# Experts of the last stage on seven tiles of 128 rows in place of eight of 112

## The chip, the cores and the metric

The kernel runs on one core of one Trainium2 chip, as one program. The metric is the device time of one execution in microseconds (us), the median of several runs.

## The reference

Eight sequences of 112 rows of 1024 floats pass through four layers, each an attention step and a feed-forward step. Only the last layer matters here:

```python
# L3 attention step: features z = layernorm(x) are gathered along the 16 nearest points
gathered = take_along_axis(feat, flat_idx, axis=2)
out = einsum('bkm,k->bm', lap, affine_w) + affine_b[0]
x = x + tanh(g_xattn[3]) * out
# L3 feed-forward step: 8 experts of rank 64, the best 2 of each row, weighted
gate_probs = softmax(x @ gate_w.T)            # x is the layernorm of the rows here
weights, sel = top_k(gate_probs, 2); weights = weights / sum(weights)
for e in range(8):
    y = x @ lora_A[e].T @ lora_B[e].T
    out = out + w_full[:, e:e + 1] * y
x = x + tanh(g_ffn[3]) * out
```

The feed-forward step treats every row by itself, so it doesn't matter which rows lie in one tile.

## The kernel before

The stages follow one another with a barrier between them. The last one, `gather_experts` (from L2814), holds both steps of the last layer. Its engines each run a loop over rounds u = 0 to 161. A round u below 128 is one of the 16 neighbours of one of the eight sequences (b = u // 16, k = u % 16). In it:

- DVE makes a one-hot matrix two rounds ahead (`marked(u + 2)`, L3088) from a row of numbers that a DMA has spread over 123 partitions, and reduces the bank of this round (`kept(u)`, L3098). `mark(n)` below is the L3088 instruction of round n.
- PE looks up with 24 small matmuls (`looked`, L2940). Every fourth round it turns four results (`turned`, L2949) and ACT copies them out (L3010).
- Every 16 rounds the table of the next sequence is made (`tabled` on PE, L2928; `split` on DVE, L298 to L307).

The spread rows come in four chunks c = 0 to 3 of a sequence, two DMAs each (912 and 72 KB), all issued by SP (`load_spread`, L292). There are two buffers, so a chunk of sequence b is issued once the rounds of sequence b - 2 have read its place, and it is first read by mark(16b + 4c).

What a sequence has gathered goes to DRAM and back: ACT stores it (L3017, round 16b + 17) and loads it again (`back_load`, L3021, round 16b + 21). PE transposes it (`returned`, L2959, in round 27 for sequence 0 and in round 16b + 25 for the others), and DVE adds it to the rows (`update`, L3107) two rounds later.

Then the experts of a sequence m run in 22 steps t, placed in round 16(m + 1) + 12 + t among the lookups of the sequences behind it. Sequence 0 has its first five steps in rounds 30, 30, 31, 31, 32, so its experts span rounds 30 to 49. The steps are: statistics (t = 0, DVE L442), root (t = 0, ACT L450), shift (t = 2, DVE L3071 to L3075), normalised rows zm (t = 3, ACT L3026), eight transposes (t = 5, PE L673) and their copies zT (t = 6, ACT L682), the gate's matmuls with 8 moving columns (t = 7, PE L2966), the matmuls h with 512 (t = 7 to 10, PE L2966), maximum, exponential and weights of the experts (t = 8 to 10), h times weights (t = 11, DVE L3151), its transposes and copy hT (t = 13, 14), the matmuls o (t = 15 to 18, PE L2966), two additions to the rows (t = 18 and 20, DVE L3158) and the store of the rows to the output (t = 21, ACT L3044). Step 21 of m and step 5 of m + 1 fall in one round; in it and the next, ACT issues the store first and then copies zT.

An f32 matmul of the code is two PE instructions. Each engine runs its instructions in the order of the loop. POOL only numbers the experts once (L2918) and is idle afterwards. The x rows of sequence 4 are loaded by ACT in round 32 (L3051), behind the root and zm of sequence 0.

Of the kernel before, what the change touches and what calls it, by code (L numbers as in the profile page):

```python
# [22 lines left out]
P = 128  # L23
# [2798 lines left out]
def gather_experts(nc, C, banks, gate, gate_ffn, x_in, x_out, A, gather, early):  # L2822
# [14 lines left out]
    with ExitStack() as ctx:  # L2837
        s_ = Scope(nc, ctx, "points")
        s_.sems += early.loaded.values()
        s_.sems += [*gather.first_loaded, gather.weights_loaded]  # L2840
        rest_x, z = s_.sb("x", [Q, B - 1, D]), s_.sb("z", [Q, 2, NA * CH])
        x = [early.sb["x0"][:]] + [rest_x[:, b, :] for b in range(B - 1)]
        consts = early.sb["consts"]
        count = consts[:, 8:9]
        norm = Norm(s_, 4)
        shift = s_.sb("shift", [Q, 4, 1])
        wsel, part = gather.wsel, gather.part
# [5 lines left out]
        gT, aT, bT = early.sb["gT"], gather.aT, gather.bT  # L2853
        zm, zT = s_.sb("zm", [Q, D]), s_.sb("zT", [P, KC, Q])
        prob, best, w8, hit = (s_.sb(n, [Q, NE]) for n in ("prob", "best", "w8", "hit"))
        place, placef, number = s_.sb("place", [Q, 8], U32), s_.sb("placef", [Q, 8]), s_.sb("number", [Q, NE])
        nmax, both = s_.sb("nmax", [Q, 1]), s_.sb("both", [Q, 1])
        h, hT = s_.sb("h", [Q, RE]), s_.sb("hT", [P, RE // P, Q])

# [7 lines left out]
        zm_ready, zT_ready, max_ready, prob_ready, h_ready, hT_ready, x_done = (  # L2867
            s_.sem(n) for n in ("zm_ready", "zT_ready", "max_ready", "prob_ready", "h_ready", "hT_ready", "x_done"))

        def steps(u):  # L2870
# [7 lines left out]

        order, nth = [], {}
        for u in range(ROUNDS):  # L2880
            b, k = u // K, u % K
            if u < U:
                order.append((("look", u), u % 3))
            if k % 4 == 1 and 1 < u <= U + 1:
                order.append((("turn", u // 4 - 1), 3))
            for m in returns(u):
                order += [(("back", m, i), 6 + i) for i in range(2)]
            if k == 13 and b + 1 < B:
                order.append((("table", b + 1), 6))
            if k == 2 and b + 1 < B:  # L2890
                nth["points", b + 1] = len(nth)
            for m, t in steps(u):
                if t == 0:
                    nth["experts", m] = len(nth)
# [21 lines left out]
        @block.gpsimd  # L2916
        def _(pool):
            pool.iota(number[:], pattern=[[1, NE]], base=0, channel_multiplier=0,  # L2918
                      allow_small_or_imprecise_dtypes=True).then_inc(numbered, 1)

        @block.tensor
        def _(pe):
# [39 lines left out]
            def part_of(t, lhsT, w, ks, n):  # L2962
                if ks[0] == 0:
                    pe.wait_ge(turns.free(t), turns.count(t, 0))
                for k in ks:
                    mm = pe.matmul(turns.tile(t)[0:Q, 0:n], lhsT[:, k, :], w(k), start=(k == 0), stop=(k == lhsT.shape[1] - 1))  # L2966
                if ks[-1] == lhsT.shape[1] - 1:
                    mm.then_inc(turns.full(t), 1)

            def experts(m, t):  # L2970
                if t == 5:
                    if m == 0:
                        pe.wait_ge(early.loaded["gT"], 16)
                        pe.wait_ge(gather.weights_loaded, 32)
                    pe.wait_ge(zm_ready, m + 1)
                    turn_rows(pe, C, turns, zm, "zT", m, 0)
                if t == 7:
                    pe.wait_ge(zT_ready, m + 1)
                    part_of(("gate", m), zT, lambda k: gT[:, k, :], list(range(KC)), NE)
                if 7 <= t < 11:  # L2980
                    part_of(("h", m), zT, lambda k: aT[:, k, :], [2 * (t - 7), 2 * (t - 7) + 1], RE)
                if t == 13:
                    pe.wait_ge(h_ready, m + 1)
                    turn_rows(pe, C, turns, h, "hT", m, 0, n=1)
                if t == 15:
                    pe.wait_ge(hT_ready, m + 1)
                if 15 <= t < 19:
# [18 lines left out]
        def _(act):  # L3006
# [16 lines left out]

            def scaled(out, src, i, n, ready):
                act.wait_ge(shift_ready, n + 1)
                act.activation(out, src, ACT.Identity, bias=shift[:, i, :], scale=norm.rstd[:, i, :]).then_inc(ready, 1)  # L3026

            def experts(m, t):
                i, n = 2 + m % 2, nth["experts", m]
                if t == 0:  # L3030
                    norm.root(act, i, n)
                if t == 3:
                    scaled(zm[:], x[m], i, n, zm_ready)
                if t == 6:
                    copy_turned(act, turns, zT, "zT", m, 0, zT_ready)
                if t == 9:
                    act.wait_ge(max_ready, m + 1)
                    act.activation(prob[:], turns.tile(("gate", m))[0:Q, 0:NE], ACT.Exp, bias=nmax[:]).then_inc(turns.free(("gate", m)), 1)
                    act.drain().then_inc(prob_ready, 1)
                if t == 14:  # L3040
                    copy_turned(act, turns, hT, "hT", m, 0, hT_ready, n=1)
                if t == 21:
                    act.wait_ge(x_done, m + 1)
                    act.dma_start(x_out[m], x[m]).then_inc(x_stored, 16)  # L3044

            for b in (1, 2):
                act.dma_start(x[b], x_in[b]).then_inc(x_loaded[b], 16)
            for u in range(ROUNDS):
# [5 lines left out]
                if k == 3 and b + 1 < B:  # L3054
                    norm.root(act, (b + 1) % 2, nth["points", b + 1])
                if k == 5 and 1 <= b <= B:
                    back_load(b - 1)
                if k == 6 and b + 1 < B:
                    scaled(z[:, (b + 1) % 2, 0:D], x[b + 1], (b + 1) % 2, nth["points", b + 1], z_ready)
                for m, t in steps(u):  # L3060
                    experts(m, t)
            act.wait_ge(x_stored, 16 * B)

        @block.vector
        def _(dve):
            def statistics(b, i):
                norm.statistics(dve, x[b], i)

            def shifted(i, n):
                dve.wait_ge(norm.std_ready, n + 1)  # L3070
# [3 lines left out]
                                         op0=ALU.mult, op1=ALU.mult)  # L3074
                dve.drain().then_inc(shift_ready, 1)  # L3075

# [25 lines left out]
            def update(b):  # L3102
                for i in range(2):
# [5 lines left out]
                       .then_inc(turns.free(t), 1)  # L3109
                dve.drain()  # L3110

            def weighed(m):
                dve.wait_ge(prob_ready, m + 1)
                dve.tensor_reduce(both[:], prob[:], AX, ALU.add)
# [12 lines left out]
                dve.drain()  # L3127
                dve.tensor_scalar(best[:, 0:2], best[:, 0:2], both[:], C.gates[0:Q, gate_ffn:gate_ffn + 1], ALU.mult, ALU.mult)
                dve.drain()
# [6 lines left out]
            def experts(m, t):  # L3136
                i, n = 2 + m % 2, nth["experts", m]
                if t == 0:
                    statistics(m, i)
                if t == 2:  # L3140
                    shifted(i, n)
                if t == 8:
                    g = ("gate", m)
                    dve.wait_ge(turns.full(g), turns.count(g, 0))
                    dve.tensor_reduce(nmax[:], turns.tile(g)[0:Q, 0:NE], AX, ALU.max, negate=True).then_inc(max_ready, 1)
                if t == 10:
                    weighed(m)
                if t == 11:
                    g = ("h", m)
                    dve.wait_ge(turns.full(g), turns.count(g, 0))  # L3150
                    dve.tensor_tensor(h[:].rearrange("q (e r) -> q e r", e=NE), turns.tile(g)[0:Q, :].rearrange("q (e r) -> q e r", e=NE),  # L3151
                                      w8[:].unsqueeze(2).broadcast_to([Q, NE, RANK]), ALU.mult).then_inc(turns.free(g), 1)
                    dve.drain().then_inc(h_ready, 1)
                if t in (18, 20):
                    g = ("o", m, (t - 18) // 2)
                    c = slice((t - 18) * 256, (t - 18) * 256 + 512)
                    dve.wait_ge(turns.full(g), turns.count(g, 0))
                    dve.tensor_tensor(x[m][:, c], turns.tile(g)[0:Q, :], x[m][:, c], ALU.add).then_inc(turns.free(g), 1)  # L3158
                    if t == 20:
# [7 lines left out]
            for u in range(ROUNDS):  # L3167
# [5 lines left out]
                if k == 2 and b + 1 < B:  # L3173
                    dve.wait_ge(x_loaded[b + 1], 16)
                    statistics(b + 1, (b + 1) % 2)
                if k == 5 and b + 1 < B:
                    shifted((b + 1) % 2, nth["points", b + 1])
                for m in returns(u - 2):
# [121 lines left out]
```

## Time and profile before

| | us |
|---|---|
| median of 3 runs | 2813.17 |
| lowest, highest | 2810.91, 2819.49 |
| span of the profiled execution | 2820.8 |
| the last stage in it | from 2479 to the end |

For the profiled execution the profile gives no time of its own beside its span; the span is above all three runs' times. Shares of the span in it: PE 92%, PEld 65%, DVE 68%, ACT 38%, POOL 20%. These are averages over stages with different limits, so the last stage has to be read by itself: by its stretches, by the chain that ended last, by DVE's timeline and by what the DMA queue of SP had moved at given moments. Times in the views are us from the start of the span.

### The profile page before, as it was taken

Reading aid. Unit: us, or ns where it says so; the run is one execution under the profiler, and the core shown is the slowest. Engines: PE = TensorE matmul, PEld = TensorE weight load, DVE = VectorE, ACT = ScalarE, POOL = GpSimd, SP = SyncE. Lnnn points to the kernel's source line nnn. Section 1 sums busy time; section 2 is a strip of 40 time slices with the busy share of each in tenths; the row PEclk is TensorE's granted clock in tenths of the full one; section 3 lists DMA queues with packets and bytes.
Section 4 is the critical chain, followed back from the end, with each engine's and each line's share of the span. In section 5 each row is a group of like instructions: output and inputs, shape, how many; then the busy total and the mean of one; then the engine's idle time right before and its main releaser. Section 6 shows DMA issues by size and latency. Waiting matters only on the chain. (4 is left out here: it accounts for less than half of the span.)

```text
span 2820.8 us, 48283 instructions
## 1 busy us (share of the span) xinstructions
PE 2583.5 (92%) x18264; PEld 1842.1 (65%) x18268; DVE 1907.7 (68%) x3366; ACT 1080.2 (38%) x2605; POOL 564.3 (20%) x602
## 2 busy tenths in 40 slices
PE   7999999999999699998899999998688999868888
PEld 5856855855865388885555555555487788556664
DVE  6376376366467677774578877777558889867774
ACT  3443434334345233332334444443255655302222
POOL 0110100001011300000045454455123334200000
PEclk9999999999999899997899999998799999989999
DMA  8011010111110745556275666544240010544421
GB/s 325 2 38 59 1 59 23 38 35 47 38 60 32 255 112 149 145 160 218 111 238 168 176 172 172 166 133 113 71 186 9 24 46 24 140 143 170 168 96 39
DMA packets 154483, 307.64 MB, mean 109 GB/s; under 512 B 84000, under 2 KB 107200, under 8 KB 144760
## 3 DMA queue, kind: packets, MB, share of 16 engines
q1 hardware_dynamic: 128952, 232.78, 25.6%
q0 software_dynamic: 19376, 57.15, 6.6%
q10 hardware_dynamic: 5936, 14.75, 1.8%
q8 instruction: 141, 2.31, 0.3%
q14 instruction: 78, 0.64, 0.1%
HBM read 249.53 MB, written 42.52 MB: 104 GB/s over the span
## 5 line engine op out<-in xcount | busy, mean ns | idle before, releaser
L1758 DVE TENSOR_REDUCE latent_nmax<-bank 112x1 f32<-112x487 f32 x128 | 85.0, 666 | 242.3 <-PE bank L1561 235.9
L1458 POOL TENSOR_SCALAR latent_probs<-latent_probs,latent_rsum 112x487 f32<-112x487 f32 x128 | 88.1, 688 | 789.6 <-DVE latent_rsum L1763 789.6
L2190 POOL TENSOR_SCALAR grouped_probs<-grouped_probs,grouped_rsum 112x375 f32<-112x375 f32 x256 | 169.6, 680 | 279.4 <-DVE grouped_rsum L2246 279.4
L2457 PE MATMUL bank<-ffn_qT,gather_whole 128*128 128x128 bf16 x3584 | 207.1, 220 | 16.7 <-ACT ffn_us L2580 6.7
L2457 PEld LDWEIGHTS bank<-ffn_qT,gather_whole 128*128 128x128 fp8e4 x3584 | 203.1, 98 | 21.7 <-issue 20.5
L2640 POOL TENSOR_TENSOR ffn_h<-ffn_sl,ffn_us 128x512 f32<-128x512 f32 x56 | 127.4, 2275 | 278.0 <-ACTq L2583 278.0
L2137 ACT ACTIVATE grouped_probs<-bank,grouped_nmax 112x375 f32<-112x375 f32 x256 | 143.3, 573 | 76.4 <-DVE grouped_nmax L2242 76.3
L2242 DVE TENSOR_REDUCE grouped_nmax<-bank 112x1 f32<-112x375 f32 x256 | 122.3, 540 | 72.2 <-PE bank L2048 69.9
L2940 PEld LDWEIGHTS bank<-gather_part,points_onehot 123*128 123x128 bf16 x3072 | 111.9, 103 | 63.1 <-DVE points_onehot L3088 32.6
L2184 POOL TENSOR_SCALAR grouped_raw<-grouped_raw,grouped_rscale 128x1024 f32<-128x1024 f32 x96 | 120.5, 1274 | 144.3 <-DVEq L2220 144.2
L2057 PEld LDWEIGHTS bank<-const_ident,grouped_probs 112*125 112x125 f32 x768 | 105.1, 196 | 67.4 <-DVE grouped_probsT L2254 28.8
L1508 PE MATMUL bank<-latent_zT,front_wq 128*128 128x224 f32 x768 | 148.0, 353 | 0.0
L1533 PE MATMUL bank<-latent_wo,latent_oT 128*128 128x512 f32 x336 | 146.6, 592 | 0.0
L1508 PEld LDWEIGHTS bank<-latent_zT,front_wq 128*128 128x128 f32 x768 | 145.0, 190 | 1.9 <-issue 1.8
L2940 PE MATMUL bank<-gather_part,points_onehot 123*128 123x63 bf16 x3072 | 117.5, 200 | 30.0 <-DVE points_onehot L3088 26.3
L2057 PE MATMUL bank<-const_ident,grouped_probs 112*125 112x112 f32 x768 | 109.8, 282 | 24.8 <-DVE grouped_probsT L2254 18.8
L1468 PE MATMUL bank<-front_wkv,front_cT 128*125 128x384 f32 x384 | 127.0, 491 | 0.0
L1468 PE MATMUL bank<-front_cT,front_wkv 128*128 128x375 f32 x384 | 123.3, 478 | 0.0
L1693 ACT ACTIVATE latent_probs<-bank,latent_nmax 112x487 f32<-112x487 f32 x128 | 85.5, 668 | 89.9 <-DVE latent_nmax L1758 82.4
L2573 ACT ACTIVATE ffn_sl<-ffn_gs,ffn_sgu 128x128 f32<-128x128 f32 x224 | 71.6, 390 | 116.5 <-DVEq L2703 116.1
L1520 PE MATMUL bank<-latent_probsT,latent_v 125*96 125x224 f32 (+1 forms) x512 | 110.2, 358 | 4.1 <-DVEq L1777 4.1
L1533 PEld LDWEIGHTS bank<-latent_wo,latent_oT 128*128 128x128 f32 x336 | 63.2, 190 | 73.9 <-issue 73.7
(435 smaller groups left out, 5576.0 us busy)
## 6 DMA issues: line engine op xcount, KB each, us to landing
grouped_raw<-L_weights SPq DMA_DIRECT2D x24, 2048.0 KB, 9.0
points_spread<-numbers SPq DMA_DIRECT2D x16, 912.0 KB
codes<-grouped_flip SPq DMA_DIRECT2D x24, 512.0 KB, 2.6
front_cT<-ctxT SPq DMA_DIRECT2D x8, 1500.0 KB, 6.8
plain_ctxT<-ctxT POOLq DMA_DIRECT2D x8, 1500.0 KB, 22.5
plain_ctx<-ctx POOLq DMA_DIRECT2D x8, 1500.0 KB, 23.4
grouped_ctx<-ctxT SPq DMA_DIRECT2D x8, 1500.0 KB, 6.7
gather_whole<-numbers SPq DMA_DIRECT2D x12, 912.0 KB
```

Source lines behind the costliest of these rows:

```text
L1468: mm = pe.matmul(turns.tile(t)[0:m, 0:n], lhsT(k), rhs(k), start=(k == 0), stop=(k == KC - 1))
L1508: mm = pe.matmul(turns.tile(t)[:, c * 2 * Q:(c + 1) * 2 * Q], wq[:, k, (2 * i + c) * P:(2 * i + c + 1) * P], zT[:, k].rearrange("p s q -> ...
L1520: mm = pe.matmul(turns.tile(t)[0:HD, 2 * half * Q:2 * (half + 1) * Q], v[0:n, k, g * HD:(g + 1) * HD], pT[0:n, half, k], start=(k == 0), s ...
L1533: mm = pe.matmul(turns.tile(t)[:], oT[:, (b - 1) % 2, k, :], wo[:, k, i * 512:(i + 1) * 512], start=(k == 0), stop=(k == OC - 1))
L2057: mm = pe.transpose(turns.tile(t)[0:CT, j * Q:(j + 1) * Q], pr[:, g % 2, j, k * CT:(k + 1) * CT], C.ident[0:Q, 0:Q])
L2137: act.activation(pr[:, i, j, :], turns.tile(t)[0:Q, 0:CTX], ACT.Exp, bias=nmax[:, i, j:j + 1], accum_out=rsum[:, i, j:j + 1]).then_inc(tur ...
L2184: pool.tensor_scalar(w, w, rscale[:, slot, i % m:i % m + 1], MAGIC, ALU.mult, ALU.add).then_inc(raw_scaled, 1)
L2190: pool.tensor_scalar(pr[:, g % 2, j, :], pr[:, g % 2, j, :], rsum[:, g % 2, j:j + 1], 1.0, ALU.mult, ALU.mult)\
L2242: dve.tensor_reduce(nmax[:, g % 2, j:j + 1], turns.tile(t)[0:Q, 0:CTX], AX, ALU.max, negate=True).then_inc(max_ready, 1)
L2457: mm = pe.matmul(ahead.tile(t)[:, i * P:(i + 1) * P], wgu[:, u0 + f // 4, c:c + 2 * P - 1:2], qT[:, k, :], start=(k == 0), stop=(k == KC - 1))
L2640: pool.tensor_tensor(h[:, G * j:G * j + G, :], sl[:, j % 2], us[:, j % 2], ALU.mult).then_inc(h_ready, 1)
L2940: mm = pe.matmul(turns.tile(t)[:, j * RA:(j + 1) * RA], onehot[0:ROWS, u % 3, j * P:(j + 1) * P], part[n][0:ROWS, b % 2, :], start=(n == 0 ...
```

## The change

The experts of sequence 0 have no steps of their own any more. Each of the seven other tiles gets 128 partitions: 112 rows of its own sequence and, in partitions 112 to 127, 16 rows of sequence 0. Once sequence 0 has its update (round 29), POOL issues seven DMAs that copy its rows there, SBUF to SBUF, 64 KB each. DVE waits for all seven ahead of the statistics of m = 1 in round 44. All operations of the experts are 128 rows wide instead of 112. Each tile is stored with two DMAs instead of one. The normalisation has buffers of its own for the experts; what the semaphores count is adapted.

```diff
-        rest_x, z = s_.sb("x", [Q, B - 1, D]), s_.sb("z", [Q, 2, NA * CH])
+        rest_x, z = s_.sb("x", [P, B - 1, D]), s_.sb("z", [Q, 2, NA * CH])
+        full = [None] + [rest_x[:, b, :] for b in range(B - 1)]
-        norm = Norm(s_, 4)
+        norm, wide = Norm(s_, 2), Norm(s_, 2, P, "wide")
-            return [(m, t) for m in range(B) for t in range(22)
-                    if u == ((30, 30, 31, 31, 32)[t] if m == 0 and t < 5 else 16 * (m + 1) + 12 + t)]
+            return [(m, t) for m in range(1, B) for t in range(22) if u == 16 * (m + 1) + 12 + t]
         @block.gpsimd
+            pool.wait_ge(first_done, 1)
+            for m in range(1, B):
+                pool.dma_start(full[m][Q:P], x[0][(P - Q) * (m - 1):(P - Q) * m]).then_inc(rows_moved, 16)
         part_of:
-                    mm = pe.matmul(turns.tile(t)[0:Q, 0:n], lhsT[:, k, :], w(k), ...)
+                    mm = pe.matmul(turns.tile(t)[0:P, 0:n], lhsT[:, k, :], w(k), ...)
-                    turn_rows(pe, C, turns, zm, "zT", m, 0)
+                    turn_rows(pe, C, turns, zm, "zT", m, 0, rows=P)
         ACT, t == 21:
                     act.dma_start(x_out[m], x[m]).then_inc(x_stored, 16)
+                    act.dma_start(x_out[0][(P - Q) * (m - 1):(P - Q) * m], full[m][Q:P]).then_inc(x_stored, 16)
         DVE, update:
-                dve.drain()
+                if b == 0:
+                    dve.drain().then_inc(first_done, 1)
+                else:
+                    dve.drain()
         DVE, experts, t == 0:
-                    statistics(m, i)
+                    if m == 1:
+                        dve.wait_ge(rows_moved, 16 * (B - 1))
+                    wide.statistics(dve, full[m], i)
```

## Rows read from the trace of the kernel before

**Rows 1.** Busy time by stretch: us, PE, PEld, DVE, ACT, POOL (instructions), clock, DMA.

```profile
2479.28:2530.40 51.12, 36.05 (x774) 32.97 (x774) 38.59 (x80) 7.03 (x11) 0.14 (x1) 0.85 0.50 164
2530.40:2543.79 13.39, 9.78 (x118) 8.98 (x119) 8.77 (x20) 1.70 (x3) 0.00 (x0) 0.56 0.41 149
2702.84:2740.02 37.18, 33.47 (x486) 23.95 (x486) 29.08 (x68) 9.50 (x14) 0.00 (x0) 1.00 0.19 60
```

**Rows 2.** The chain that ended last: start, us, what; two transfers, then the tail.

```profile
2487.55 37.97 DMA points_spread<-numbers
...
2554.43 10.16 DMA points_back<-flat
...
2796.45 0.33 ACTq L3044
2796.83 0.54 ACT points_zT L682
```

**Rows 3.** DMA queue q1 (SP's): packets, MB from 2484.6 to 2533.4, 2544.8, 2564.7.

```profile
q1 hardware_dynamic: 817, 5.96, 35.6%
q1 hardware_dynamic: 1033, 7.55, 36.3%
q1 hardware_dynamic: 1330, 9.70, 35.4%
```

**Rows 4.** The same queue in 2566 to 2582 and in 2582 to 2604.

```profile
q1 hardware_dynamic: 307, 2.25, 38.2%
q1 hardware_dynamic: 338, 2.47, 30.8%
```

**Rows 5.** DVE's timeline: start, us, what, count, idle before it and its releaser.

```profile
2533.39 0.48 DVE L3088 TENSOR_SCALAR points_onehot<-gather_whole,points_consts 123x1024 bf16<-123x1024 bf16 x1 [0.79 <-DMA gather_whole<-numbers]
2538.91 1.29 DVE L442 BATCH_NORM_STATS2 points_ln_stats<-points_x 112x6 f32<-112x512 f32 x2
2540.63 0.48 DVE L3088 TENSOR_SCALAR points_onehot<-gather_whole,points_consts 123x1024 bf16<-123x1024 bf16 x1
2564.69 0.49 DVE L3088 TENSOR_SCALAR points_onehot<-gather_whole,points_consts 123x1024 bf16<-123x1024 bf16 x1
2568.65 0.68 DVE L3098 TENSOR_REDUCE points_val<-bank 128x56 f32<-128x504 f32 x1 [3.47 <-PE bank L2940]
2579.42 0.68 DVE L3098 TENSOR_REDUCE points_val<-bank 128x56 f32<-128x504 f32 x1 [1.77 <-PE bank L2940]
2581.86 0.69 DVE L3158 TENSOR_TENSOR points_x<-bank,points_x 112x512 f32<-112x512 f32 x1
```

**Rows 6.** ACT's timeline around the first store of gathered rows of sequence 1.

```profile
2529.21 0.59 ACT L3010 ACTIVATE points_flat<-bank 56x512 f32<-56x512 f32 x1 [8.54 <-PE bank L2949]
...
2542.30 0.31 ACTq L3051 DMA_DIRECT2D points_x<-x  x1
2544.21 0.32 ACTq L3017 DMA_DIRECT2D flat<-points_flat  x1
```

**Rows 7.** PE's timeline: the gate's matmuls and h of sequence 1.

```profile
2588.05 1.72 PE L2966 MATMUL bank<-points_gT,points_zT 128*112 128x8 f32 x16
2589.62 1.95 PE L2966 MATMUL bank<-gather_whole,points_zT 128*112 128x512 f32 x4
```

**Rows 8.** PE instructions by line, ns min/median/max: 112 and 128 stationary columns.

```profile
L2966 PEld LDWEIGHTS bank<-gather_whole,points_zT x128: 176/177/310, 2548.4 to 2805.6; 128*112 128x112 f32 x128
L2966 PE MATMUL bank<-gather_whole,points_hT x128: 592/592/815, 2569.6 to 2815.2; 128*112 128x512 f32 x128
L1533 PEld LDWEIGHTS bank<-latent_wo,latent_oT x336: 187/190/192, 211.6 to 918.8; 128*128 128x128 f32 x168
L1533 PE MATMUL bank<-latent_wo,latent_oT x336: 590/592/608, 211.7 to 919.2; 128*128 128x512 f32 x168
```

**Rows 9.** The dearest kind of DMA issue on POOL (1.5 MB each), ns min/median/max.

```profile
L755 POOL DMA_DIRECT2D plain_ctx<-ctx x8: 1307/1319/1342, 976.4 to 1242.7; - x8
```

**Rows 10.** The way back of gathered rows (L3021, 448 KB), from issue to landing.

```profile
DMA to landing us min/median/max: 3.1/9.0/10.2
```

More of the change, by code:

```diff
@@ L2840, in gather_experts @@
         s_.sems += [*gather.first_loaded, gather.weights_loaded]
-        rest_x, z = s_.sb("x", [Q, B - 1, D]), s_.sb("z", [Q, 2, NA * CH])
-        x = [early.sb["x0"][:]] + [rest_x[:, b, :] for b in range(B - 1)]
+        rest_x, z = s_.sb("x", [P, B - 1, D]), s_.sb("z", [Q, 2, NA * CH])
+        x = [early.sb["x0"][:]] + [rest_x[0:Q, b, :] for b in range(B - 1)]
+        full = [None] + [rest_x[:, b, :] for b in range(B - 1)]
         consts = early.sb["consts"]
         count = consts[:, 8:9]
-        norm = Norm(s_, 4)
-        shift = s_.sb("shift", [Q, 4, 1])
+        norm, wide = Norm(s_, 2), Norm(s_, 2, P, "wide")
+        shift, wide_shift = s_.sb("shift", [Q, 2, 1]), s_.sb("wide_shift", [P, 2, 1])
         wsel, part = gather.wsel, gather.part
@@ L2853, in gather_experts @@
         gT, aT, bT = early.sb["gT"], gather.aT, gather.bT
[L2854 to L2858, printed above, removed]
+        zm, zT = s_.sb("zm", [P, D]), s_.sb("zT", [P, KC, P])
+        prob, best, w8, hit = (s_.sb(n, [P, NE]) for n in ("prob", "best", "w8", "hit"))
+        place, placef, number = s_.sb("place", [P, 8], U32), s_.sb("placef", [P, 8]), s_.sb("number", [P, NE])
+        nmax, both = s_.sb("nmax", [P, 1]), s_.sb("both", [P, 1])
+        h, hT = s_.sb("h", [P, RE]), s_.sb("hT", [P, RE // P, P])
         numbered = s_.sem("numbered")
@@ L2889, in gather_experts @@
                 order.append((("table", b + 1), 6))
-            if k == 2 and b + 1 < B:
-                nth["points", b + 1] = len(nth)
             for m, t in steps(u):
-                if t == 0:
-                    nth["experts", m] = len(nth)
                 if t == 5:
@@ L2965, in part_of @@
                 for k in ks:
-                    mm = pe.matmul(turns.tile(t)[0:Q, 0:n], lhsT[:, k, :], w(k), start=(k == 0), stop=(k == lhsT.shape[1] - 1))
+                    mm = pe.matmul(turns.tile(t)[0:P, 0:n], lhsT[:, k, :], w(k), start=(k == 0), stop=(k == lhsT.shape[1] - 1))
                 if ks[-1] == lhsT.shape[1] - 1:
@@ L2982, in experts @@
                 if t == 13:
-                    pe.wait_ge(h_ready, m + 1)
-                    turn_rows(pe, C, turns, h, "hT", m, 0, n=1)
+                    pe.wait_ge(h_ready, m)
+                    turn_rows(pe, C, turns, h, "hT", m, 0, n=1, rows=P)
                 if t == 15:
-                    pe.wait_ge(hT_ready, m + 1)
+                    pe.wait_ge(hT_ready, m)
                 if 15 <= t < 19:
@@ L3022, in back_load @@
                               flat_dram[b % 2].rearrange("a c -> (a c)").rearrange("(p c) -> p c", p=P)).then_inc(back_loaded[b % 2], 16)
-            def scaled(out, src, i, n, ready):
-                act.wait_ge(shift_ready, n + 1)
-                act.activation(out, src, ACT.Identity, bias=shift[:, i, :], scale=norm.rstd[:, i, :]).then_inc(ready, 1)
             def experts(m, t):
-                i, n = 2 + m % 2, nth["experts", m]
+                i = m % 2
                 if t == 0:
-                    norm.root(act, i, n)
+                    wide.root(act, i, m - 1)
                 if t == 3:
-                    scaled(zm[:], x[m], i, n, zm_ready)
+                    act.wait_ge(wide_shift_ready, m)
+                    act.activation(zm[:], full[m], ACT.Identity, bias=wide_shift[:, i, :], scale=wide.rstd[:, i, :]).then_inc(zm_ready, 1)
                 if t == 6:
-                    copy_turned(act, turns, zT, "zT", m, 0, zT_ready)
+                    copy_turned(act, turns, zT, "zT", m, 0, zT_ready, rows=P)
                 if t == 9:
-                    act.wait_ge(max_ready, m + 1)
-                    act.activation(prob[:], turns.tile(("gate", m))[0:Q, 0:NE], ACT.Exp, bias=nmax[:]).then_inc(turns.free(("gate", m)), 1)
+                    act.wait_ge(max_ready, m)
+                    act.activation(prob[:], turns.tile(("gate", m))[0:P, 0:NE], ACT.Exp, bias=nmax[:]).then_inc(turns.free(("gate", m)), 1)
                     act.drain().then_inc(prob_ready, 1)
                 if t == 14:
-                    copy_turned(act, turns, hT, "hT", m, 0, hT_ready, n=1)
+                    copy_turned(act, turns, hT, "hT", m, 0, hT_ready, n=1, rows=P)
                 if t == 21:
-                    act.wait_ge(x_done, m + 1)
+                    act.wait_ge(x_done, m)
                     act.dma_start(x_out[m], x[m]).then_inc(x_stored, 16)
+                    act.dma_start(x_out[0][(P - Q) * (m - 1):(P - Q) * m], full[m][Q:P]).then_inc(x_stored, 16)
             for b in (1, 2):
@@ L3054, in _ @@
                 if k == 3 and b + 1 < B:
-                    norm.root(act, (b + 1) % 2, nth["points", b + 1])
+                    norm.root(act, (b + 1) % 2, b)
                 if k == 5 and 1 <= b <= B:
@@ L3058, in _, with shifted @@
                 if k == 6 and b + 1 < B:
-                    scaled(z[:, (b + 1) % 2, 0:D], x[b + 1], (b + 1) % 2, nth["points", b + 1], z_ready)
+                    i = (b + 1) % 2
+                    act.wait_ge(shift_ready, b + 1)
+                    act.activation(z[:, i, 0:D], x[b + 1], ACT.Identity, bias=shift[:, i, :], scale=norm.rstd[:, i, :]).then_inc(z_ready, 1)
                 for m, t in steps(u):
                     experts(m, t)
-            act.wait_ge(x_stored, 16 * B)
+            act.wait_ge(x_stored, 2 * 16 * (B - 1))
         @block.vector
         def _(dve):
-            def statistics(b, i):
-                norm.statistics(dve, x[b], i)
-            def shifted(i, n):
+            def shifted(norm, shift, ready, i, n):
                 dve.wait_ge(norm.std_ready, n + 1)
@@ L3127, in weighed @@
                 dve.drain()
-                dve.tensor_scalar(best[:, 0:2], best[:, 0:2], both[:], C.gates[0:Q, gate_ffn:gate_ffn + 1], ALU.mult, ALU.mult)
+                dve.tensor_scalar(best[:, 0:2], best[:, 0:2], both[:], C.gates[:, gate_ffn:gate_ffn + 1], ALU.mult, ALU.mult)
                 dve.drain()
@@ L3136, in experts @@
             def experts(m, t):
-                i, n = 2 + m % 2, nth["experts", m]
+                i = m % 2
                 if t == 0:
-                    statistics(m, i)
+                    if m == 1:
+                        dve.wait_ge(rows_moved, 16 * (B - 1))
+                    wide.statistics(dve, full[m], i)
                 if t == 2:
-                    shifted(i, n)
+                    shifted(wide, wide_shift, wide_shift_ready, i, m - 1)
                 if t == 8:
@@ L3144, in experts @@
                     dve.wait_ge(turns.full(g), turns.count(g, 0))
-                    dve.tensor_reduce(nmax[:], turns.tile(g)[0:Q, 0:NE], AX, ALU.max, negate=True).then_inc(max_ready, 1)
+                    dve.tensor_reduce(nmax[:], turns.tile(g)[0:P, 0:NE], AX, ALU.max, negate=True).then_inc(max_ready, 1)
                 if t == 10:
@@ L3150, in experts @@
                     dve.wait_ge(turns.full(g), turns.count(g, 0))
-                    dve.tensor_tensor(h[:].rearrange("q (e r) -> q e r", e=NE), turns.tile(g)[0:Q, :].rearrange("q (e r) -> q e r", e=NE),
-                                      w8[:].unsqueeze(2).broadcast_to([Q, NE, RANK]), ALU.mult).then_inc(turns.free(g), 1)
+                    dve.tensor_tensor(h[:].rearrange("q (e r) -> q e r", e=NE), turns.tile(g)[0:P, :].rearrange("q (e r) -> q e r", e=NE),
+                                      w8[:].unsqueeze(2).broadcast_to([P, NE, RANK]), ALU.mult).then_inc(turns.free(g), 1)
                     dve.drain().then_inc(h_ready, 1)
@@ L3157, in experts @@
                     dve.wait_ge(turns.full(g), turns.count(g, 0))
-                    dve.tensor_tensor(x[m][:, c], turns.tile(g)[0:Q, :], x[m][:, c], ALU.add).then_inc(turns.free(g), 1)
+                    dve.tensor_tensor(full[m][:, c], turns.tile(g)[0:P, :], full[m][:, c], ALU.add).then_inc(turns.free(g), 1)
                     if t == 20:
@@ L3174, in _ @@
                     dve.wait_ge(x_loaded[b + 1], 16)
-                    statistics(b + 1, (b + 1) % 2)
+                    norm.statistics(dve, x[b + 1], (b + 1) % 2)
                 if k == 5 and b + 1 < B:
-                    shifted((b + 1) % 2, nth["points", b + 1])
+                    shifted(norm, shift, shift_ready, (b + 1) % 2, b)
                 for m in returns(u - 2):
```

12 lines of the change are left out of this document (6 added, 6 removed).

## The prediction

> **What bounds the kernel now.** I read the stage from its start on 2479 by stretches, then the chain, then DVE's timeline and SP's queue.
>
> PE is the busiest engine of the last stage: 33.5 of 37.2 us in a full period of 16 rounds with experts, DVE 29.1 beside it [rows 1]. Neither is full, but they hand work to each other every round, so the period is long by both. From this view the experts of one sequence look like a big prize. They are 16 h and 16 o instructions and 16 gate instructions. The gate takes 2589.62 - 2588.05 = 1.57 us for 16 [rows 7]; a big one is spaced 0.45 us (four last 1.95, one alone 0.59 [rows 7, 8], so three spacings are 1.36), which makes 32 x 0.45 + 1.6 = 16 us, and about 1.5 us for 12 transposes: some 17.5 us of PE.
>
> The experts of sequence 0 don't lie in such a period, though. They lie in rounds 30 to 49, from 2538.91 [rows 5] to shortly before the gate of sequence 1 at 2588.05 [rows 7], and that stretch has another limit. The first third of the stage is led by the spread rows: the chain holds a transfer of 38 us [rows 2], PE was busy 36.1 of 51.1 us [rows 1], and mark(32) at 2533.39 still waited for its chunk [rows 5]. A chunk is 123 rows of 8 KB, 1.01 MB. When mark(32) was let go, five chunks had landed, 5.04 MB, and q1 had moved 5.96 MB [rows 3]: the queue runs 0.92 MB ahead of what is complete. From there to 2564.7 it moved 9.70 - 5.96 = 3.74 MB in 31.3 us [rows 3], 0.12 MB/us, with its share of the engines constant at 35 to 36%. So the stream never pauses, and it can't be hurried by reading earlier.
>
> How far is the stream ahead of the marks? At 2544.8 (mark(36), chunk 6 needed, 6.05 MB) it stands 7.55 - 6.05 - 0.92 = 0.58 MB ahead, 4.8 us. At 2564.69 (mark(44), 8 chunks, 8.06 MB [rows 5]) it is 9.70 - 8.06 - 0.92 = 0.72 MB, 6 us [rows 3]. The lead within the queue may well be larger than 0.92 MB there, as it varies; with 1.2 MB these are 2.5 and 3.7 us. So the rounds that lose their experts can come forward by 3 to 6 us until round 42, and not more. Behind that the slack grows by itself, since a period with experts takes 37 us [rows 1] and its four chunks 4.03/0.12 = 34.
>
> **The change part by part.** Taken against the profiled execution, 2820.8 us of span, whose difference I then put on the median of the runs, 2813.2; the two differ by 7.6 us, which is the run and not a stage that I can name.
>
> *Removed in rounds 30 and 31.* DVE loses the statistics of sequence 0, 2540.63 - 2538.91 = 1.7 us [rows 5], and the shift. PE stands at 0.56 of its clock there, that is mostly at 1.2 GHz [rows 1], and a lookup then takes about 1.3 us, so only some 1.1 us reach the store of the gathered rows at 2544.21 [rows 6]. Without root and zm ahead of it the load of x rows at 2542.30 moves forward to ACT's last copy, near 2530, and away from that store [rows 6]. The way back of what was stored was issued at 2554.43 [rows 2], so the store had at most 10.2 us for its 448 KB. Transfers of that size took 3.1 to 10.2 us, the median 9.0 [rows 10]. With no neighbour of ACT's I take 8 for the store, from 2543.1 to 2551.1, and 9.0 for the way back: it lands at 2560.1 instead of 2564.6.
>
> *The stream's new neighbours.* In 2566 to 2582 q1 ran alone at 2.25/16 = 0.141 MB/us, in 2582 to 2604 with four transfers of ACT at 2.47/22 = 0.112 [rows 4]: 22 x 0.029 = 0.64 MB less, 1.1 us for each transfer of 448 KB. The seven DMAs of POOL are together one such transfer, and start before 2533, after the update that precedes mark(32) [rows 5]. The moved load of x is another for chunks 6 and 7. So chunk 8 lands 1.1 us later than now: mark(44) comes forward by 3.7 - 1.1 = 2.6 us, at most 4.9.
>
> *Rounds 42 to 49.* Now kept(42) comes at 2568.65, 3.5 us late for PE [rows 5], and 4.1 us after the way back has landed (2554.43 + 10.16 [rows 2]); of these some 0.8 are four transposes of h at the low clock, which go. So it comes at 2560.1 + 3.3 = 2563.4, right behind mark(44) at 2562.1: 5.2 us earlier. Behind it go the wait of 1.77 us at 2579.42 for the o matmuls, and two additions of 0.69 us with 0.14 of gap each [rows 5]: 5.2 + 1.8 + 1.7 = 8.7 us. Against it stands PE's clock, which falls after idle time; if it is at 1.2 GHz for a part of this, rounds of 1.22 us become 1.3 and the table is twice as dear. I take off 1.2: **7.5 us gained by round 50**, bounds 4 and 9.
>
> *128 rows instead of 112.* DVE's work doesn't change with partitions. The big matmuls cost the same, 592 ns at 112 and at 128 stationary columns [rows 8]. The gate is paced by its weight loads, 98 ns each; loads grow from 177 to 190 ns [rows 8], so 16 x 13 = 0.21 us per tile. Transposes move 16 more columns, 0.45 us/512 x 16 = 14 ns each by 12, of which half lie on the chain, 0.08. The copies of zT and hT grow from 448 columns in 0.54 us [rows 2] toward the 512 in 0.59 of another copy [rows 6], 0.05 each.
>
> *The second store.* It is one more issue of 0.33 us with a gap of 0.05 in ACT's queue, ahead of the copies of zT of the next tile. This lies on the chain: 2796.45 store, 2796.83 copy [rows 2], and in the periods too the gate waits for these copies. So m = 2 to 7 pay 0.38 + 0.10 on the way to the gate, m = 1 doesn't (no store is ahead of it). Sum per tile: m = 1 0.3; m = 2 to 5 0.78 each, 3.1; m = 6 and 7 in the tail, with nothing to hide behind, 0.9 each, 1.8; the last store 0.38. That is 5.6 us. In the periods PE also waits for DVE, which hides some; I take 4.8, bounds 3 and 6.
>
> *The move itself.* POOL has nothing else queued. Seven issues of 1.32 us, as the dearest were [rows 9], are 9.2 us, and a transfer of 448 KB is 9 [rows 10], so the move ends by 2552; DVE asks for it in round 44, near 2568. It costs nothing as long as those 16 us cover it. If they don't, DVE stands with every mark and kept of the later rounds behind the wait, and PE behind those.
> The rows show POOL's issues only at moments that don't tell how busy DVE's second port was. The Trainium skill (SBUF — State Buffer, "SBUF: two separate sides") says that descriptors of POOL's DMAs can't be written while DVE runs in a two-port mode, and names 620 ns growing to 3100. An estimate by that page is 7 x 3.1 = 22 us, which would still be hidden; no row here shows the blocking.
>
> **Sum:** 7.5 - 4.8 = 2.7 us less: 2818.1 of span, 2810.5 as median.
>
> **The rivals.**
> *The stream doesn't bind.* If it can be hurried or the lead is smaller, rounds 34 to 50 run at DVE's pace: 16 rounds in 29.1 us, its busy time in a full period [rows 1], less 3.5 for the part of the expert steps that goes, plus 3 of gaps, so 17 in 30.4. Now they take 43.3, from 2544.8 to 2588.05. That gains 13, less 4.8: 8.2, 2805.0. For it speaks PE's and DVE's load; against it the constant 35% of q1.
> *Nothing is left.* PE at 1.2 GHz through the thinned rounds (it had 0.56 in 2530 to 2544 [rows 1]) and all of the width's cost on the chain: 4 - 6, 2 us slower, 2815.
> *Slower: the move is late.* The wait in round 44 decides from 2568 on, 35 us after the update, or 5 us for each of the seven DMAs. Each us beyond is lost in full. With 8 us each (the descriptors starved between DVE's marks) it ends at 2588.6, 20 us late, 17 net: 2830. Against it: 1.32 us per issue at most [rows 9], and DVE idles a quarter of the stretch. The page named above is the rule behind this rival.
>
> **How the numbers follow.** Forecast 0.60; stream doesn't bind 0.17; nothing left 0.18; move late 0.05. Own range of the forecast, 4 - 6 to 9 - 3: 2807 to 2815. The range for 8 in 10 takes in most of the first rival and what the runs differ by: 2803.0 to 2816.5. Within 0.3% (8.4 us, about what a measurement of this kernel can tell from no change) lie the forecast and the third case. Faster by more: the first rival from its middle on and a tail of the forecast, 0.16. Slower by more: the late move and a bit, 0.06.
>
> **What would show it.** Right: mark(40) or mark(44) waits for a DMA of numbers; the way back of sequence 1 lands about 2559; the first gate starts 8 us before 2588; the gap between store and copy of zT holds a second issue; gates take 1.8 us; later periods are 0.5 to 0.8 us longer. Wrong: no DMA wait in rounds 34 to 46 and a start of the gate 12 us early (first rival); a PE clock of a half from 2550 to 2575; a wait of DVE before L442 of m = 1 for the row copies.

## The result and the profile after

The changed kernel is slower: 2827.9 us against 2818.7 (medians of 20 runs each), a ratio of 1.0035 with a 95% interval of 1.0023 to 1.0047. The forecast was 2.7 us less; it came out some 10 us more, 0.35%. The median before of 20 runs, 2818.7, is itself 5.5 us above the median of three runs, 2813.2, on which the prediction put its range of 2803.0 to 2816.5. So its times in us were set too low from the start; the difference between the kernels is what the rest is about.

The two profiles don't show this at first sight. The span of the profiled execution is 2819.0 us after and 2820.8 before. Single executions of either kernel lie within 21 to 25 us of each other (before 2807.3 to 2832.0, after 2819.6 to 2840.6), and here a quick execution of the changed kernel was caught beside a rather slow one of the old. So I give a second profile of each in the view that matters: the last stage cut into a front (from its start to the gate of m = 1), a middle (to the gate of m = 6) and a tail. Columns: stretch, us, busy us and instructions of PE, PEld, DVE, ACT, POOL, then clock, DMA share, GB/s.

The kernel before, the profile that the prediction read:

```profile
2479.36:2588.05 108.69, 84.63 (x1435) 71.16 (x1435) 78.08 (x171) 19.62 (x30) 0.14 (x1) 0.84 0.49 165
2588.05:2774.59 186.54, 165.76 (x2322) 118.23 (x2318) 138.88 (x322) 46.06 (x68) 0.00 (x0) 0.98 0.36 124
2774.59:2820.80 46.21, 37.78 (x120) 18.71 (x120) 12.96 (x42) 7.89 (x11) 0.00 (x0) 0.91 0.15 43
```

The kernel before, a second profile (e5 below), cut at the same gates:

```profile
2481.20:2583.70 102.50, 82.07 (x1435) 68.60 (x1435) 78.16 (x171) 19.63 (x30) 0.12 (x1) 0.86 0.51 172
2583.70:2766.40 182.70, 163.25 (x2322) 115.74 (x2317) 138.79 (x322) 46.07 (x68) 0.00 (x0) 1.00 0.37 128
2766.40:2812.50 46.10, 37.62 (x120) 18.71 (x120) 12.96 (x42) 7.89 (x11) 0.00 (x0) 0.91 0.16 44
```

The kernel after, its profile:

```profile
2477.53:2576.10 98.57, 67.37 (x1374) 62.78 (x1375) 71.95 (x148) 13.84 (x22) 3.55 (x8) 0.80 0.52 171
2576.10:2766.62 190.52, 167.66 (x2323) 120.69 (x2319) 138.03 (x322) 46.83 (x68) 0.00 (x0) 0.99 0.37 129
2766.62:2819.00 52.38, 43.16 (x120) 22.75 (x120) 12.94 (x42) 8.11 (x11) 0.00 (x0) 0.83 0.11 37
```

The kernel after, a second profile (e1 below):

```profile
2480.40:2583.30 102.90, 70.31 (x1374) 64.94 (x1374) 71.89 (x148) 13.83 (x22) 3.55 (x8) 0.78 0.53 166
2583.30:2775.20 191.90, 169.31 (x2319) 121.49 (x2316) 138.01 (x322) 46.84 (x68) 0.00 (x0) 0.98 0.37 128
2775.20:2824.80 49.60, 40.37 (x120) 20.91 (x120) 12.95 (x42) 8.11 (x11) 0.00 (x0) 0.88 0.12 39
```

The front went from 102.5 or 108.7 to 98.6 or 102.9 us, with 12 to 17 us less of PE's time busy in it: by these four alone it is shorter by up to 10 us or not at all. The middle went from 182.7 or 186.5 to 190.5 and 191.9, and the tail from 46.1 and 46.2 to 52.4 and 49.6. Nothing of the experts of sequence 0 was ever in these two. That is 4 to 9 us in the middle and 3 to 6 in the tail, though two profiles of each don't size it: single executions differ there too (table behind the experiments).

What grew there stands in ACT's timeline at the place that [rows 2] showed for before. After, from the store of gathered rows (L3017) to the copies of zT, ahead of the gate of m = 3:

```profile
2649.70 0.33 ACTq L3017 DMA_DIRECT2D flat<-points_flat  x1
2650.29 0.33 ACTq L3041 DMA_DIRECT2D x_final<-points_x  x1
2650.65 1.36 ACTq L3042 DMA_DIRECT2D x_final<-points_x  x1
2652.05 1.09 ACT L682 ACTIVATE points_zT<-bank 128x512 f32<-128x512 f32 x2 [2.46 <-issue]
```

The second store (L3042) holds ACT for 1.36 us, not for 0.33. Of all seven, first the two stores of a tile after (ns min/median/max of the issue), then the single one of before:

```profile
L3041 ACTq DMA_DIRECT2D x_final<-points_x x7: 322/328/1320, 2611.7 to 2814.6; - x7
L3042 ACTq DMA_DIRECT2D x_final<-points_x x7: 445/1357/1948, 2613.0 to 2814.9; - x7
```

```profile
L3044 ACTq DMA_DIRECT2D x_final<-points_x x8: 328/328/373, 2586.2 to 2816.6; - x8
```

In the first of the seven tiles it was the other way round: the first store took 1.32 us and the second 0.45. The other six second stores took 1.36, 1.62, 1.69 and 1.95 us, and 0.45 twice.

And the chain that ended last, after, where the tail begins:

```profile
2762.68 0.33 ACTq L3017
2763.05 0.37 ACTq L3041
2763.45 1.95 ACTq L3042
2765.40 0.05 issue
2765.45 0.60 ACT points_zT L682
2766.04 0.53 ACTq L684
2766.62 13.39 PE bank L2966 x32
```

The issue of 1.95 us lies on the chain, and PE waits for it: its waits for the drain behind the copies (L684) are 10.8 us in the stage, against 4.0 in before.

```profile
PE bank L2966 <- ACTq L684: 10.8, 8, 3.7
```

```profile
PE bank L2966 <- ACTq L684: 4.0, 4, 1.8
```

The tail after is granted 0.83 of the clock in one profile and 0.88 in the other, against 0.91 in both of before. How much of this follows from the waits is taken up below.

### The profile page after: what moved, and what is told of

The parts are those of the page before. It is cut to its first block and busy times, and to the rows that moved or that the text cites. A ratio compares the mean times of both kernels' runs of the same rounds, so it can differ in the third digit from the quotient of the medians.

```text
span 2819.0 us, 48123 instructions
## 1 busy us (share of the span) xinstructions
PE 2572.6 (91%) x18204; PEld 1838.7 (65%) x18208; DVE 1900.4 (67%) x3343; ACT 1074.0 (38%) x2597; POOL 566.0 (20%) x609
## 5 line engine op out<-in xcount | busy, mean ns | idle before, releaser
L3095 DVE TENSOR_REDUCE points_val<-bank 128x56 f32<-128x504 f32 x128 | 86.8, 678 | 39.0 <-PE bank L2940 38.8
```

## The experiments

Ratios are against the kernel before, run on the same chip in turn; 0.001 is 2.8 us. A difference in us behind a ratio is worked out from the ratio. e1 to e4 shared one chip, e5 to e8 a second, e9 to e12 a third.

**e1, the changed kernel again.**

> The changed kernel once more, as the yardstick for the other three and for a second profile. Issue theory (the second store of a tile stands in ACT's queue ahead of the copies of zT, with an issue of 1.3 to 2.0 us where 0.38 was reckoned): ratio about 1.003, again five issues of L3042 over 1.3 us, and a step of over 1.5 us from x_done to the first copy of zT for m = 3 to 6. Clock theory (the thinned rounds and the longer waits lower PE's clock): the ratio is the same, but the low-clock time of the last stage differs from profile to profile and the time goes with it.

Measured: 2826.2 us, 1.0029 (1.0015 to 1.0043). Its second stores took 0.81, 1.54, 1.71, 1.77, 1.95, 0.45 and 0.45 us to issue. So four lie over 1.3 us. I expected five "again", but the first profile had four at L3042 as well; its fifth slow one was a first store. The result of the first runs holds. The low-clock theory isn't excluded by this run alone.

**e2, the second store from POOL.**

```diff
-                    act.dma_start(x_out[0][...], full[m][Q:P]).then_inc(x_stored, 16)
+            for m in range(1, B):          # POOL, behind the move
+                pool.wait_ge(x_done, m)
+                pool.dma_start(x_out[0][...], full[m][Q:P]).then_inc(rows_stored, 16)
```

> The second store of each tile is issued by POOL, on a semaphore of its own, and no longer by ACT. Everything else as in the changed kernel, and the output is complete. Issue theory: the 0.45 + 4 x 1.5 us of issue leave ACT's queue; 6 to 8 us less than the changed kernel, about 2820, ratio to before 1.000. Clock or width theory: no change against the changed kernel, ratio 1.003.

Measured: 2818.2 us, 0.9993 (0.9980 to 1.0007). This interval lies apart from that of e1. Moving seven issues of 64 KB from one queue to another takes back 0.36%, 10 us by the ratios and 8 by the medians. One first store, still issued by ACT, took 1.36 us (m = 1, at 2622.75), with no second one behind it. POOL's issue is short every time, and the middle and the tail are near the size of e5's:

```profile
L2922 POOL DMA_DIRECT2D x_final<-points_x x7: 484/484/487, 2623.0 to 2811.6; - x7
```

```profile
2586.70:2769.90 183.20, 165.54 (x2319) 119.59 (x2316) 138.11 (x322) 46.85 (x68) 2.43 (x5) 1.00 0.38 134
2769.90:2817.20 47.30, 37.04 (x120) 18.68 (x120) 12.96 (x42) 8.11 (x11) 0.97 (x2) 0.92 0.16 46
```

**e3, no second store.** The line is left out, and POOL stores sequence 0 once after its update.

> The second stores are left out; sequence 0 is stored once by POOL straight after its update, so its rows in the output are without the experts' part. The move and the 128 rows stay. Issue theory: as with POOL's stores, 6 to 8 us below the changed kernel; what is between the two is the price of the transfers themselves, 0 to 1 us. Width theory: still at or above the kernel before.

Measured: 2815.5 us, 0.9993 (0.9978 to 1.0007), the same ratio as e2. The transfers cost nothing that shows; what cost was where they were issued. The profile is of the slowest of its twelve runs (2827.6) and is a warning: its middle is 193.0 us long without any second store, with two periods of over 41 us at a granted clock of 0.92.

**e4, the gain alone.** 112 rows everywhere, no move, no second store.

```diff
-        rest_x, z = s_.sb("x", [P, B - 1, D]), ...
+        rest_x, z = s_.sb("x", [Q, B - 1, D]), ...
-                turn_rows(pe, C, turns, zm, "zT", m, 0, rows=P)      # and so on for all experts' tiles
+                turn_rows(pe, C, turns, zm, "zT", m, 0)
+            pool.dma_start(x_out[0], x[0]).then_inc(rows_stored, 16)
```

> The experts of sequence 0 are simply left out (its rows in the output are without their part, stored once by POOL after the update); the seven other tiles stay at 112 rows, with no move and no second store. This is the gain alone. My sum: 7.5 us below the kernel before, 2811, ratio 0.997; bounds 4 and 9, and 13 if the stream of spread rows doesn't bind. The difference to the run without second stores is the width and the move: my sum 2 to 2.5 us. Clock theory: less than 4 us below before, with a low-clock time of the last stage 10 us above before's 55.

Measured: 2812.7 us, 0.9982 (0.9966 to 0.9998). The gain of leaving out an eighth of the experts is 5 us, with an interval from 0.6 to 9.6; the medians differ by 7.2. So neither my sum of 7.5 nor the clock theory's "less than 4" can be told from it. The front is 96.0 us in its profile, the middle 189.6. The expectation of 13 us if the stream of spread rows didn't bind is excluded by the interval.

**e5, the kernel before again, one run.**

> The kernel before, unchanged, for a second profile of it: when does the gate of m = 1 start, counted from the start of the last stage (109 us in the first profile, 96 to 103 in the four kernels without experts of sequence 0), and which periods hold a spell of low clock (41 us with one, 37 without)? Both theories expect 105 to 112 us and one or two long periods.

Measured: 2814.1 us in its one run. The gate of m = 1 starts 102.5 us into the stage, below the range that I expected, and no period is long. This suggests that the profile that the prediction read was an unlucky one in its front: 108.7 us. The other kernels with all eight tiles have 102.7 (e7), 105.4 (e8, which clears zm first), 102.7 (e10) and 102.5 (e12).

**e6, both stores behind the copies of zT.**

```diff
                 if t == 6:
                     copy_turned(act, turns, zT, "zT", m, 0, zT_ready, rows=P)
+                    if m > 1:
+                        stored(m - 1)        # the two stores of t == 21
```

> The changed kernel, complete, with both stores of a tile issued by ACT behind the two copies of zT of the next tile instead of ahead of them. Issue theory: the slow issue (1.4 to 2.0 us as the third transfer that ACT issues within a microsecond) no longer stands before the gate, so 7 to 10 us below the changed kernel, ratio to before 0.999. If the transfer itself is the cost (its share of the queue), nothing changes: 1.003.

Measured: 2813.3 us, 0.9987 (0.9969 to 1.0006). The same bytes go from the same queue, 1.2 to 1.4 us later, and 0.42% is back (against e1, on another chip; the intervals lie apart). It has the lowest ratio of the complete kernels, though its interval holds no change, and e2, e11 and e12 can't be told from it. Five of the seven second stores took 0.45 us, one 0.72 and one 1.62, though these two came about 2 us behind the store of gathered rows:

```profile
L3047 ACTq DMA_DIRECT2D x_final<-points_x x7: 450/451/1625, 2619.9 to 2806.9; - x7
```

**e7, a split store alone.** The kernel before, with one more issue per tile and nothing else.

```diff
-                    act.dma_start(x_out[m], x[m]).then_inc(x_stored, 16)
+                    act.dma_start(x_out[m][0:Q - 16], x[m][0:Q - 16]).then_inc(x_stored, 16)
+                    act.dma_start(x_out[m][Q - 16:Q], x[m][Q - 16:Q]).then_inc(x_stored, 16)
```

> The kernel before with the store of each tile as two DMAs, 96 and 16 rows, in ACT's queue where the one was; nothing else changes, the bytes and rows are the same. Issue theory: the second issue takes 1.4 to 2.0 us in the middle tiles, and the kernel is 8 to 10 us slower, ratio 1.003. If the width or the move was the cause: 1.000.

Measured: 2829.1 us, 1.0048 (1.0028 to 1.0068): 13.5 us for splitting eight stores (7.9 to 19.2). This is at least the loss of the changed kernel, within the noise, with none of its other parts. The second issues took 0.59, 0.83, 1.60, 2.71, 1.77, 2.02, 0.44 and 0.45 us: the first two are shorter than expected, the fourth is longer. ACT's timeline in the worst tile:

```profile
2697.49 0.33 ACTq L3017 DMA_DIRECT2D flat<-points_flat  x1
2698.11 0.33 ACTq L3044 DMA_DIRECT2D x_final<-points_x  x1
2698.47 2.71 ACTq L3045 DMA_DIRECT2D x_final<-points_x  x1
2701.23 0.98 ACT L682 ACTIVATE points_zT<-bank 128x448 f32<-128x448 f32 x2 [3.84 <-issue]
```

Its front is as before, its middle is 195.6 us long and its tail 47.1:

```profile
2478.10:2580.80 102.70, 80.41 (x1435) 67.03 (x1435) 78.36 (x171) 19.60 (x30) 0.14 (x1) 0.88 0.51 170
2580.80:2776.40 195.60, 168.81 (x2316) 119.43 (x2316) 138.42 (x322) 46.02 (x68) 0.00 (x0) 0.97 0.36 122
2776.40:2823.50 47.10, 37.92 (x120) 18.82 (x120) 12.95 (x42) 7.89 (x11) 0.00 (x0) 0.90 0.12 37
```

**e8, the width alone.** The kernel before, with zm, zT, prob, h and hT of 128 rows; all eight tiles are 128 wide from the transposes to the o matmuls.

> The kernel before with all experts 128 rows wide from the transposes on (rows 112 to 127 of zm are zero, the additions stay at 112 rows): eight tiles, the width alone. My sum: 0.3 to 0.45 us for each of eight tiles, 3 us, ratio 1.001. Width theory: 8 us or more, 1.003.

Measured: 2819.4 us, 1.0010 (0.9994 to 1.0025), 2.8 us, as summed, though the interval holds zero too. The loss of 10 us is outside of it.

**e9, the small store first.** The two lines of t = 21 change places.

> The changed kernel with the 64 KB store of a tile ahead of the 448 KB one; both stay ahead of the copies of zT. Issue theory, in the form that the third transfer issued by ACT in about a microsecond is the slow one whatever its size: the small store now takes 0.33 us and the big one behind it 1.4 to 2.0, and the ratio stays at 1.003. If the slow issue belongs to transfers of 16 rows, the small one stays slow in first place and the big one takes 0.4.

Measured: 2825.6 us, 1.0023 (1.0005 to 1.0042). The 64 KB store, now L3041, is quick, and the 448 KB store behind it is the slow one:

```profile
L3041 ACTq DMA_DIRECT2D x_final<-points_x x7: 321/327/373, 2613.8 to 2823.8; - x7
L3042 ACTq DMA_DIRECT2D x_final<-points_x x7: 439/1558/1772, 2614.1 to 2824.1; - x7
```

So it isn't the 16 rows: here the slow issue is the third of ACT's in a row, and not the small one. In all these kernels the last two tiles, which have no store of gathered rows right ahead, pay 0.44 or 0.45 us for the second one.

**e10, the move alone.**

```diff
+            pool.wait_ge(first_done, 1)
+            for m in range(1, B):
+                pool.dma_start(full[m][Q:P], x[0][...]).then_inc(rows_moved, 16)
```

> The kernel before with only the move added: POOL copies the rows of sequence 0 into partitions 112 to 127 of the seven other tiles after its update, and nothing reads them; DVE waits for the move ahead of the first addition to sequence 0, in round 46. My sum: the spread stream loses 1.1 us, hidden or nearly; ratio 1.000, at most 1.001. Late-move theory: 1.003 and more.

Measured: 2820.8 us, 1.0010 (0.9993 to 1.0026). In its profile (span 2810.4) DVE never waits for the move. The interval reaches from 2 us gained to 7 lost, so whether the move costs something these runs can't tell.

**e11, both stores from POOL.** As e2, with `pool.dma_start(x_out[m], x[m])` ahead of the other.

> The changed kernel, complete, with both stores of a tile issued by POOL. ACT issues no store any more and starts the copies of zT 0.4 us earlier than in the kernel before. Issue theory: the best of all, 0.38 us for each of six tiles below the run with only the second store on POOL: 2 us less, ratio 0.998 to 0.999. If POOL's transfers were starved by DVE, the last one would land late and the end would be 1 to 5 us later.

Measured: 2816.2 us, 0.9991 (0.9975 to 1.0007). POOL's issues took 0.50 to 0.55 us. The 2 us beyond e2 that were expected can't be told from the noise.

**e12, the kernel before with late stores.** As e6, for the one store of before.

> The kernel before with its single store of a tile behind the copies of zT of the next tile. It shows what moving the stores gives without the change of tiles: 0.38 us for each of seven tiles, 2 to 3 us, ratio 0.999. The changed kernel with late stores then stands against this one for the fewer tiles: my sum for that is 5 gained (the run without experts of sequence 0) less 3 for the width.

Measured: 2813.9 us, 0.9990 (0.9975 to 1.0005). It stands beside e6 (0.9987): with the stores out of the way in both, tiles of 128 rows and eight tiles of 112 can't be told apart. The difference that I had put at 2 us is there or not within the noise.

**All profiles side by side.** The kernels that have ACT issue two stores ahead of the copies of zT are the last four rows. Middle: from the gate of m = 1 to that of m = 6. Last period: from the gate of m = 5 to that of m = 6. Waits: PE at the gate and the o matmuls for ACT's drain (L684), in the whole stage.

| profile | middle, us | last period, us | waits, us |
|---|---|---|---|
| before, e5 | 186.5, 182.7 | 32.7, 32.7 | 4.0, 4.0 |
| e4, e10, e12 | 189.6, 183.5, 181.8 | 32.7, 32.7, 32.3 | 4.0, 4.0, 3.4 |
| e8, e2, e3 | 182.9, 183.2, 193.0 | 33.0, 33.0, 33.0 | 4.1, 4.7, 4.7 |
| e6, e11 | 183.3, 184.3 | 32.6, 32.6 | 3.5, 3.5 |
| after, e1 | 190.5, 191.9 | 35.0, 36.7 | 10.8, 10.5 |
| e7, e9 | 195.6, 197.6 | 34.8, 34.9 | 11.3, 10.7 |

The middle alone doesn't part the two kinds: e3 and e4 have long ones with no second store, in periods whose clock fell to 0.92 to 0.96. The waits and the last period do part them, in every profile: 6 to 8 us more of waits, and 1.8 us or more in the last period.

## Why the prediction was wrong

**The step that failed is "the second store".** The prediction found its place rightly: in ACT's queue, ahead of the copies of zT, with the gate behind them on the chain. It priced it wrongly, with the 0.33 us of an issue and a gap, taken from a row of a queue in which two transfers follow one another. Where a store of gathered rows had just been issued, the second store was the third issue in a row and mostly took 1.4 to 2.0 us. I had 0.38 for each of the stores, 2.7 us in all. Undoing it is worth 8 to 12 us (e1 or the first runs against e2), and adding it alone to the kernel before costs 13.5 (e7). The direct part is the issues themselves: the seven sum to 8.0 us in the profile after and to 8.7 in e1, six of them ahead of a gate, and PE's waits for ACT grew by 6 to 8 us. That a rest of some us is PE's clock, lower after the longer waits, is argued and not shown.

This also hit the range: it had a rival with the width's costs all on the chain, but none in which an issue costs more than every issue of its kind in the trace. The bounds for a new operation were taken from its like, not from what surrounds it. The trace of before had a warning in another queue: SP's issues of spread rows, one behind the other, took from 0.26 to 11.2 us each, eight of them 3.44 us at the start of the stage and the next eight 33.7.

```profile
L292 SPq DMA_DIRECT2D points_spread<-numbers x32: 258/502/8549, 2484.6 to 2693.5; - x32
L292 SPq DMA_DIRECT2D gather_whole<-numbers x24: 295/2291/11222, 2488.1 to 2655.0; - x24
```

**The gain in the front may have been too big.** The sum had 7.5 us with bounds 4 and 9; e4 measures 5 (0.6 to 9.6), which holds both. The limit was seen rightly. In the profile after, mark(40) and mark(44) wait for their chunks, 0.21 and 4.22 us, as the working had said of the stream. All eight profiles without experts of sequence 0 have such a wait at mark(44), 3.3 to 4.2 us, and none of the six with them has one. In the profile after PE also waits 7.07 us for the way back, and DVE behind it for PE:

```profile
2544.77 0.49 DVE L3085 TENSOR_SCALAR points_onehot<-gather_whole,points_consts 123x1024 bf16<-123x1024 bf16 x1 [0.21 <-DMA gather_whole<-numbers]
...
2553.72 0.49 DVE L3085 TENSOR_SCALAR points_onehot<-gather_whole,points_consts 123x1024 bf16<-123x1024 bf16 x1 [4.22 <-DMA gather_whole<-numbers]
2558.19 0.68 DVE L3095 TENSOR_REDUCE points_val<-bank 128x56 f32<-128x504 f32 x1 [3.98 <-PE bank L2940]
```

What was missed is that the front of the profile before was itself long, 108.7 us, where four others have 102.5 to 102.7 and a fifth 105.4. So part of what was to be won may be there in some executions only. Against 102.5 the eight profiles without experts of sequence 0 have fronts of 96.0 to 102.9 us, 99.5 in the mean. The term for PE's clock had its place: these eight fronts were granted 0.76 to 0.80 of it, the six others 0.84 to 0.88, and from 2550 to 2575 it was 0.66 in the profile after against 0.86 before. That lies between what I had seen and the clock of a half that I had named as a sign of the second rival.

**The width was right.** 16 gate instructions take 1.79 us instead of the 1.57 of [rows 7], 0.22 more where 0.21 was worked out, and h and o keep their 592 ns. e8 measures 2.8 us for eight tiles, with an interval from 2 us gained to 7 lost.

```profile
2576.11 1.93 PE L2966 MATMUL bank<-points_gT,points_zT 128*128 128x8 f32 x16
2577.90 0.68 PE L2966 MATMUL bank<-gather_whole,points_zT 128*128 128x512 f32 x1
```

**The move came in time, as predicted.** POOL issues its seven DMAs in 3.4 us, each cheaper than [rows 9]; they land 2.8 to 11.1 us later, and DVE has no wait for them ahead of the statistics of m = 1.

```profile
L2919 POOL DMA_DIRECT2D points_x<-points_x x7: 484/487/522, 2529.4 to 2532.4; - x7
```

The blocking of which the Trainium skill warns (SBUF — State Buffer, "SBUF: two separate sides"), with its 620 ns growing to 3100, doesn't show in these issues: the longest took 522 ns, beside a DVE that was busy for 12.4 of 16.3 us. Whether DVE was in the two-port mode that the page asks for no view shows.

**The sum with the measured terms:** 5 gained, 2.5 for the width of seven tiles, 0 to 3 for the move: from 2.5 less to 0.5 more, and e2 has 2 less (0.9993, an interval that holds zero). With the second store on ACT, 8 to 12 more: 5.5 to 12.5 above before, and 10 was measured. Each term has an interval of several us, so the sum agrees but doesn't prove the single terms.

## What to carry to other kernels

An added DMA is priced by its place in its queue as much as by its size: when two transfers already follow one another there, look for what a third does, or try one alone, before taking the duration of the others for it, and look up the longest issue in every queue of the trace. Put stores behind the work on whose result another engine waits; that costs a few lines and took back here what the added store had cost, within the noise. Where single executions differ by more than the effect, take a second profile of the kernel before, since a stretch that looks slow in one may be the clock of that execution.

## What the runs showed of the hardware

- The issue of a DMA can hold the engine that gives it. Where ACT issued a store of gathered rows and two more stores right behind it (after, e1, e7, e9), the third took 1.36 to 2.71 us in 17 of 21 cases and 0.45 to 0.83 in four; the first two took 0.32 to 0.37 but for one of 1.32. It didn't depend on whether the third was 64 or 448 KB (e9), nor on SP: in the profile after SP's last issue ends at 2681.8, and ACT's of 1.62, 1.69 and 1.95 us come at 2690.75, 2728.67 and 2763.45. With the copies of zT in between, three of five took 0.45, the others 0.72 and 1.62 (e6). From POOL the same store took 0.48 each time (e2).
- Three in a row are neither enough nor needed. At the start of the stage before, ACT issues three loads of 448 KB in 1.3 us, two in 0.83 together and the third in 0.45. And a first store took 1.32 (after), 1.36 (e2) and 1.38 us (e3), each in the tile of m = 1, where the same place of before took 0.33. SP's issues in before lasted up to 11.2 us. What is full at such a moment no view shows; it stays open.
- PE starts the gate of m = 6 at the low clock after its wait: its 16 instructions last 3.58 us in the profile after and 3.15 in the one of before, where the gate of m = 1 lasts 1.93 and 1.72. With tiles of 128 rows the 32 instructions of gate and h of m = 6 took 12.2 to 13.5 us in the three profiles with the longer wait (after, e1, e9) and 8.9 to 10.6 in the five without (e2, e3, e6, e8, e11). With 112 rows no such difference shows: 11.96 in e7, and 10.39 to 12.02 in the five others. So what the longer wait costs beyond itself is open.
